# Attention scores from two rounded fp32 parts, with even and odd heads in the two halves of the array's rows

## The reference

```
x      = layernorm(input)                       # before the attention
Q,K,V  = x @ Wq.T + bq, x @ Wk.T + bk, x @ Wv.T + bv
scores = Q K^T / sqrt(16) + prior_lambda * mask(|i - j|)   # mask is a band, cut at 59 off the diagonal
attn   = softmax(scores);  out = attn V
x1     = input + (heads joined) @ Wo.T + bo
```

## Time and profile before

| what | value |
|---|---|
| median of 3 runs | 6518.96 us (6516.07 to 6520.48) |
| the profiled execution | 6517.32 us, its span 6515.5 us, 1.8 us lie around it |
| PE busy | 6199.8 us, 95% |
| DVE busy | 5158.3 us, 79% |
| ACT busy | 3831.1 us, 59% |
| attention, its 1024 steps | about 123.6 to 3571.2 us of the span |
| PE's granted clock | 1.00 of 2.4 GHz in nearly all of it |

### The profile page before, as it was taken

The page is one execution under the profiler, slowest core; times in us unless marked ns, Lnnn a source line. Parts: engine busy times, 40 slices in busy tenths (PEclk is TensorE's granted clock), DMA queues, the critical chain, the costliest instruction groups (busy, mean ns, idle before and its releaser), DMA issues. The chain is left out here.

```text
span 6515.5 us, 109356 instructions
## 1 busy us (share of the span) xinstructions
PE 6199.8 (95%) x42144; PEld 3462.2 (53%) x42336; DVE 5158.3 (79%) x10993; ACT 3831.1 (59%) x6282; POOL 1584.7 (24%) x1131
## 2 busy tenths in 40 slices
PE   7999999999999999999999799999899899999899
PEld 2333233333332333333322588888788688888788
DVE  6888888888888888788886788888666788888666
ACT  2665665666656656656666466666333566666332
POOL 0000000000000000000000577777200577777211
PEclk7999999999999999999999899999999899999999
DMA  1111111111111111111100100000000100000111
GB/s 47 20 25 28 20 25 42 22 32 19 28 36 22 29 29 19 25 38 24 24 16 9 48 15 13 15 15 10 26 12 4 33 15 15 13 15 9 54 49 43
DMA packets 150862, 160.14 MB, mean 25 GB/s; under 512 B 26268, under 2 KB 135620, under 8 KB 150340
## 3 DMA queue, kind: packets, MB, share of 16 engines
q1 hardware_dynamic: 150340, 153.14, 10.1%
HBM read 68.38 MB, written 16.78 MB: 13 GB/s over the span
## 5 line engine op out<-in xcount | busy, mean ns | idle before, releaser
L548 ACT ACTIVATE a_pr<-a_w 128x1024 f32<-128x1024 f32 x2048 | 2076.4, 1023 | 1124.9 <-PE a_w L423 800.2
L678 DVE TENSOR_REDUCE a_mx<-a_b 128x1 f32<-128x512 f32 x2688 | 1739.5, 684 | 332.0 <-PE a_b L407 312.6
L407 PE MATMUL a_b<-a_kp,a_qp 96*128 96x512 bf16 x4096 | 1449.9, 388 | 120.4 <-DVE a_mx L678 47.8
L423 PE MATMUL a_w<-a_qp,a_kp 99*128 99x512 bf16 x4096 | 1224.7, 380 | 32.6 <-ACT a_pr L548 32.5
L676 DVE CUSTOM_DVE_ANT_0 a_junk<-a_b,a_gw 128x512 bf16<-128x512 f32 x1408 | 964.4, 685 | 230.3 <-PE a_b L407 195.8
L454 PE MATMUL a_po<-a_pr,a_v 128*17 128x512 f32 x8192 | 1068.3, 595 | 0.5 <-ACT a_pr L548 0.5
L407 PEld LDWEIGHTS a_b<-a_kp,a_qp 96*128 96x128 bf16 x4096 | 339.7, 97 | 1238.5 <-issue 656.9
L1398 POOL TENSOR_TENSOR l_p<-l_p,l_rc 128x512 f32<-128x512 f32 (+1 forms) x512 | 633.0, 1260 | 450.7 <-DVE l_rc L1311 450.7
L1205 ACT ACTIVATE l_p<-l_S,l_nm 128x256 f32<-128x256 f32 (+1 forms) x1024 | 467.1, 465 | 458.6 <-DVE l_nm L1303 458.6
L423 PEld LDWEIGHTS a_w<-a_qp,a_kp 99*128 99x128 bf16 x4096 | 388.1, 98 | 513.9 <-ACT a_pr L548 108.8
L1054 PE MATMUL l_G<-l_wqkv,l_hT 128*128 128x512 f32 x2304 | 607.4, 409 | 21.8 <-DVE l_wqkv L1343 9.3
(11 more groups left out here) (164 smaller groups left out, 8302.8 us busy)
## 6 DMA issues: line engine op xcount, KB each, us to landing
a_xc<-in_x SPq DMA_DIRECT2D x60, 512.0 KB
a_qp<-a_qs SPq DMA_DIRECT2D x384, 64.0 KB, 2.4
a_kp<-a_ks SPq DMA_DIRECT2D x384, 64.0 KB, 2.4
l_tab<-in_rotary SPq DMA_DIRECT2D x128, 128.0 KB, 2.1
x<-a_xc SPq DMA_DIRECT2D x16, 512.0 KB, 2.9
f_xo<-x SPq DMA_DIRECT2D x16, 512.0 KB
out<-xs SPq DMA_DIRECT2D x16, 512.0 KB, 3.2
l_sh<-xs SPq DMA_DIRECT2D x32, 224.0 KB
```

The lines of the kernel that those rows point to most:

```text
L407: eng.matmul(bk, qp[s][0:96, qb * 128:qb * 128 + 128], kp[s][0:96, c * 512:c * 512 + 512], start=True, stop=True).then_inc(full, 1)
L423: m = eng.matmul(wide[u][:, c * 512:c * 512 + 512], kp[s][0:99, kb * 128:kb * 128 + 128], qp[s][0:99, u * 1024 + c * 512:u * 1024 + c * 51 ...
L548: eng.activation(pr[(2 * n + u) % NP][:, :], wide[u][:, :], ACT.Exp, scale=0.25).then_inc(s_exp[u], 1)
L678: t = eng.tensor_reduce(mx[g % 2][:, qb, c:c + 1], banks[i], X, ALU.max)
```

## The change

q and k are split into two fp32r parts instead of three bf16 parts. Three products (`QPART`, `KPART`) make 48 contraction rows, and 50 with the two rows of the negated maximum. Heads alternate between partitions 0 to 63 and 64 to 127 of the operand buffers (`operands(g)`), of which there are now two pairs of 128 rows, which hold four heads. PE's order alternates one pass-1 matmul and one pass-2 matmul; the unit stands in the middle of the step, and `band` and `pv` at its end.

`project` is ACT (fp32 copy with bias), ACT (the same, rounded to fp32r) and POOL (the difference), and then a DMA of 512 KB to a DRAM tensor that keeps the parts of all heads of all batches. `pack(g)` reads from there by 6 DMAs of 128 KB. x is loaded, normalized and turned once per batch; from that one pass come the values and all four projections of a chunk. The units of the next batch are spread from step 32 of the batch on, one about every fourth step. The first batch's projections of both groups of heads all stand before the steps.

```diff
-QPART = [0, 1, 2, 0, 1, 0]
-KPART = [0, 0, 0, 1, 1, 2]
+QPART = [0, 0, 1]
+KPART = [0, 1, 0]
...
+ROWS = 3 * DA
...
+def chunk_units(b, j):
+
+    return ([("turned", b, j, half) for half in range(2)] + [("values", b, j, half) for half in range(2)]
+            + [("project", b, c, j, n) for c in range(2) for n in "qk"])
...
-        n = n0 + 85
-        for j in range(4):
-            for what in (("turned", b, 1, j, 0), ("turned", b, 1, j, 1), ("project", b, 1, j, "q"), ("project", b, 1, j, "k")):
-                n = plan(n, *what)
...
-            n = n0 + 114
+            n = n0 + 32
             for j in range(4):
-                n = plan(n, "stats", b + 1, j) + 2
...
+                n = plan(n, "stats", b + 1, j) + 3
+                for what in chunk_units(b + 1, j):
+                    n = plan(n + 3, *what) + 1
...
-    parts = {"q": sb("qs", [128, 3, L], BF16), "k": sb("ks", [128, 3, L], BF16)}
-    qp = [sb(f"qp{i}", [128, L], BF16) for i in range(3)]
-    kp = [sb(f"kp{i}", [128, L], BF16) for i in range(3)]
+    parts = {n: nc.dram_tensor(n + "_parts", [NB, 2, 2, 128, L], F32, kind="Internal").ap() for n in "qk"}
+    stage = [sb(f"stage{i}", [128, 2, 512], F32R) for i in range(2)]
+    qp = [sb(f"qp{i}", [128, L], F32R) for i in range(2)]
+    kp = [sb(f"kp{i}", [128, L], F32R) for i in range(2)]
...
+    def operands(g):
+
+        return qp[g // 2 % 2], kp[g // 2 % 2], 64 * (g % 2)
...
         def pass1(n, c):
...
-                pe.wait_ge(s_pack[s], PACK * (g // 3 + 1))
-                eng.matmul(bk, qp[s][0:96, qb * 128:qb * 128 + 128], kp[s][0:96, c * 512:c * 512 + 512], start=True, stop=True).then_inc(full, 1)
...
+                pe.wait_ge(s_pack[g % 4], PACK * (g // 4 + 1))
+                eng.matmul(bk, q[r:r + ROWS, qb * 128:qb * 128 + 128], k[r:r + ROWS, c * 512:c * 512 + 512], start=True, stop=True).then_inc(full, 1)
...
         for n in range(-LEAD, NS + 1):
-            pass1(n, 0)
-            pass2(n, halves_of(n)[0])
-            pass1(n, 1)
-            pass2(n, halves_of(n)[1])
-            pass1(n, 2)
+            for c in range(2):
+                pass1(n, c)
+                pass2(n, halves_of(n)[0], c)
+            if n in units and units[n][0] in work:
+                work[units[n][0]](units[n])
+            for c in range(2):
+                pass1(n, c + 2)
+                pass2(n, halves_of(n)[1], c)
             band(n)
             pv(n - 1)
-            if n in units and units[n][0] in work:
-                work[units[n][0]](units[n])
-            pass1(n, 3)
...
+            act.wait_ge(s_full[i], k)
+            if m > 2:
+                act.wait_ge(s_lo, m - 2)
+                act.wait_ge(s_part[(m - 1) % 2], 16 * ((m - 1) // 2))
+            eng.activation(tmp[(m - 1) % 2][:, :], banks[i], ACT.Identity, bias=bias[n][:, c:c + 1]).then_inc(s_whole, 1)
+            eng.activation(stage[(m - 1) % 2][:, 0, :], banks[i], ACT.Identity, bias=bias[n][:, c:c + 1]).then_inc(s_free[i], 1)
...
-                dve.wait_ge(s_dve, step.on(eng.tensor_tensor(r1[:, :], nm[:, :], pk[:, 0, :], ALU.subtract)))
-                dve.wait_ge(s_dve, step.on(eng.tensor_copy(pk[:, 1, :], r1[:, :])))
-                eng.tensor_tensor(pk[:, 2, :], r1[:, :], pk[:, 1, :], ALU.subtract).then_inc(s_pk, 1)
+                eng.tensor_tensor(pk[:, 1, :], nm[:, :], pk[:, 0, :].bitcast(F32), ALU.subtract).then_inc(s_pk, 1)
...
+            eng.dma_start(parts[n][b, c, :, :, j * 512:j * 512 + 512].rearrange("t p n -> p t n"), stage[(m - 1) % 2][:, :, :].bitcast(F32)).then_inc(s_part[(m - 1) % 2], 16)
...
+            for n, dst, order in (("q", q, QPART), ("k", k, KPART)):
                 for j, p in enumerate(order):
-                    eng.dma_start(dst[16 * j:16 * j + 16, :], parts[n][r0:r0 + 16, p, :]).then_inc(s_pack[s], 16)
+                    eng.dma_start(dst[r + 16 * j:r + 16 * j + 16, :].bitcast(F32), parts[n][b, h // 8, p, r0:r0 + 16, :]).then_inc(s_pack[g % 4], 16)
```

More of the change, by code:

```diff
@@ L196, in unit @@
             return
[L197 removed]
+        if (what[0] == "turned" and what[3] == 0) or (what[0] == "out_T" and what[2] % 4 == 0):
             n_hT += 1
@@ L212, in attention_tables @@
     for half in range(2):
-        tick("normed", ("turned", 0, "v", 0, half))
+        tick("normed", ("turned", 0, 0, half))
     for j in range(4):
[L215 to L218, removed]
+        of_chunk = chunk_units(0, j)
+        for what in of_chunk:
             unit(what, 7)
@@ L222, in attention_tables @@
             for half in range(2):
-                tick("normed", ("turned", 0, "v", j + 1, half))
-        for what in held:
-            rest(what)
+                tick("normed", ("turned", 0, j + 1, half))
+        for what in of_chunk:
+            if what[0] in HOLDS:
+                rest(what)
     before_main = list(t.n)
@@ L245, in attention_tables @@
                 after = units[n]
[L246 to L249, removed]
+        for c in range(2, 4):
+            if p1:
+                t.take(("p1", g1, qb, c), 3)
+        if p1 and qb == W - 1:
+            later.append(("rows", g1))
         if n > 0 and n % W == 0:
@@ L471, in tensor @@
         for j in range(4):
-            for half in range(2):
-                turned(("turned", 0, "v", j, half))
-            for half in range(2):
-                values(("values", 0, j, half))
-            for n in "qk":
-                project(("project", 0, 0, j, n))
+            for what in chunk_units(0, j):
+                work[what[0]](what)
         pe.wait_ge(s_ones, 1)
@@ L509, in turned @@
         def turned(what):
-            half = what[4]
+            half = what[3]
             i, k = slot[what]
@@ L746, in vector @@
                 for half in range(2):
-                    normal(("turned", 0, "v", j + 1, half))
-            for n in "qk":
-                project(("project", 0, 0, j, n))
-        dve.wait_ge(s_setup, 3)
+                    normal(("turned", 0, j + 1, half))
+        dve.wait_ge(s_setup, 2)
         after = norm = None
@@ L807, in gpsimd @@
                 rstd(rs[:, 4 * j + 4:4 * j + 8], 4)
-            for n in "qk":
-                project_lo(("project", 0, 0, j, n))
+            for what in chunk_units(0, j):
+                if what[0] == "project":
+                    project_lo(what)
         after = None
@@ L894, in sync @@
         for j in range(4):
-            turned(("turned", 0, "v", j, 1))
+            turned(("turned", 0, j, 1))
+            for what in chunk_units(0, j):
+                if what[0] == "project":
+                    project(what)
+        sp.wait_ge(s_ones, 1)
         pack(0)
@@ L905, in sync @@
             if after:
-                store(after)
-                norm, after = after, None
+                if after[0] == "project":
+                    project(after)
+                else:
+                    store(after)
+                    norm = after
+                after = None
             if n in units:
```

192 lines of the change are left out of this document (75 added, 117 removed).

## The result

The changed kernel takes 6562.4 us, the median of 7 runs (6551.68 to 6605.92); the kernel before, measured beside it, takes 6518.7 us, the median of 7 (6516.07 to 6520.48). The ratio is 1.0076, with a 95% interval of 1.0052 to 1.0101: slower, where I forecast 6265 and faster. The time lies inside the range of 6110 to 6600, but on the wrong side of 6519: that it lies there is no merit of the mechanism. The profiled execution's span is 6560.6 us, 45.1 above that of before.

What follows compares the result with a forecast made beforehand. PE's stream was taken as the bound, with DVE close. From 6517.3 us, plain heads -119, units -107, output units -19 and work before the steps -8 gave 6264, stated as 6265; range 6110 to 6600.

Steps and rivals of the forecast that it cites:

- the halves overlap: Score matmuls in rows 0 to 63 and 64 to 127 run at the same time; plain heads shorten, -119 us.
- DVE releases the loop: In plain steps, a loop from DVE's first chunk through the three banks becomes the bound, 2.70 us a step.
- The extras: Per head, waits at the change of halves and the turns of maxima and finished head: 2.3 us kept as 2.4.
- Weights at nothing: In score matmuls, fp32r weight loads of 0.188 us against bf16's 0.10 stay hidden, so the difference costs nothing.
- before the steps: Ahead of the attention steps, eight more projections and their stores add +15 us, ends +8 and +25.
- The forecast sum of 41 us for a spread set: The next batch's units in the steps cost 41 us a set, 36 less than before; three times, -107 us.
- the sentence on new waits: ACT's two projection copies after both exponentials delay the next ones about 0.7 us, inside slack; all waits zero, up to +20.
- My own sign of being wrong: Wrong if pairs start 0.23 apart, ACT bounds the step, or a project unit costs more than 1.5 us.
- The worst case of the forecast: In the spread sets, each unit costs its present 1.5 us and only 16 dropped turned a batch gain: -38 us.
- the first rival: The halves of the rows don't overlap, every step is 2.99 us: 6585 us, slower; chance 0.17.
- the clock, given 0.04: In the steps, PE rests and its clock falls; with a third of steps slow, 6630 us; chance 0.04.
- the output sets: The 16 output units stay together and cost 29 us a set instead of 35.3: -19 us, ends 0 and -40.

Runs made afterwards that it cites:

- The inline kernel: Changed kernel, but ACT and DVE take a unit's result from its bank within the same step and the bank is not held over; 6440.0 us, ratio 0.988.
- the kernel with ACT's part alone: Changed kernel, but only ACT takes a unit's result between the two exponentials; DVE's takes and the holding of banks stay; 6539.6 us, ratio 1.0031.
- the second experiment: Changed kernel, but PE repeats a 50-row pass-2 matmul before each of the third and fourth pass-1 matmuls; 6756.3 us, ratio 1.0375.
- in the first: Changed kernel, but consecutive heads lie in the same half of the rows and every second pair of heads in the other; 6822.1 us, one run.
- consecutive steps: Changed kernel, but the next batch's units stand in consecutive steps instead of every fourth; 6528.8 us, ratio 1.0014.
- the two together: The inline kernel with the next batch's units in consecutive steps; 6439.7 us, ratio 0.9876.
- unit at the end: Changed kernel, but the unit stands behind pv at the end of PE's step instead of in the middle; 6520.8 us, ratio 1.0005.
- inline, whole array: The inline kernel plus two bf16 matmuls of 512 columns on all 128 rows in eleven of a head's steps; 6706.9 us, ratio 1.0289.
- inline, half array: The inline kernel plus two repeats of the 50-row pass-2 matmul in eleven of a head's steps; 6479.8 us, ratio 0.9938.

## Why the prediction was wrong, point by point

**Right: the halves overlap, and DVE releases the loop.** Pairs start together. A plain step is 2.75 (forecast 2.70), the last key block with both matmuls in one half 3.08 (2.99), a plain head 47.1 (46.5). The extras are 2.1 instead of 2.4. That rows overlap at all was taken without a row that showed it, and it came true in full. The last 0.05 is in the loop's small terms: 0.43 instead of 0.41 from the fourth pair to `band`, 0.17 instead of 0.16 from DVE to the pair. Weights at nothing was right, in a same-half stretch too: 0.23 between matmuls with their loads between. Only the first pair after `pv` took 0.11 more, outside the loop. This part gave 83 of the forecast 119 us.

**Right in kind: before the steps.** +18.5 us against +15, inside 8 to 25.

**Wrong: the units, the largest term.** The forecast sum of 41 us for a spread set priced a unit's own step only. The medians at full clock, over a plain step:

| unit | count | forecast | own step | step behind | measured |
|---|---|---|---|---|---|
| project | 16 | 1.2 | 1.55 | 0.45 | 2.0 |
| values | 8 | 1.6 | 1.6 | 1.5 | 3.1 |
| turned | 8 | 0.5 | 1.0 | 0.8 | 1.8 |
| stats | 4 | 1.3 | 0.45 | 1.2 | 1.6 |

They sum to 32 + 25 + 14 + 6 = 77.6 us, just what the kernel before paid for its unit sets (76.8). (Three of the four stats stand in the step behind a projection, so that some 1 us of the sum is counted twice.) Three sets miss by 110 us, about 90 of it in the steps behind. The step that failed is the sentence on new waits, that ACT's two copies come behind both exponentials "inside their slack": they delay no exponential much, but hold one of three banks over the step's end, and pass 1 needs it. The same holds of values, which DVE takes in the next step: the forecast priced them at 1.6 in all, and they cost 3.1. My own sign of being wrong, a project unit above 1.5 us, came true with 2.0. The inline kernel takes the steps behind projections, values and `turned` down to plain ones, and the kernel with ACT's part alone those behind projections and `turned`, and so they show the cause. The worst case of the forecast was also mis-summed: 16 dropped units at 1.5 us are 24 a batch, 72 us for three, not 38; the first rival's 6585 has the same 38.

**Wrong: the clock, given 0.04.** The sets measured 324 us where full clock makes 233, so 91 us are the clock's in these alone; with the output sets and single heads I put it at some 110 to 125, from some 80 steps with low clock, of which some 60 had no unit and took 4.4 us on average, where a plain step takes 2.75. My argument against it was that PE would be full at 1.2 GHz and that this would bring the clock back. The window 700 to 724 has PE busy all the time at 0.50, so it doesn't hold. My picture of the cause, PE resting, did not hold either: the second experiment filled most of the rests and had 342 us, and in the first the clock fell behind 15 us of which PE rested 0.7. The rival's size was guessed at a third of all steps; it was some 80 of 1024, and so turned the sign only together with the units.

The mean granted clock of every run confirms this size. The traces here have the two levels 0.50 and 1.00 only, so that it gives the time at 1.2 GHz in the whole execution, layers behind the attention included: 2 x (1 - clock) x span.

| kernel | runs | median us | at 1.2 GHz, median us |
|---|---|---|---|
| before (profiled run) | 1 | 6517.3 | 221 |
| changed | 7 | 6562.4 | 525 |
| both passes in one half | 1 | 6822.1 | 928 |
| more score matmuls | 4 | 6756.3 | 554 |
| inline | 4 | 6440.0 | 412 |
| ACT's part only | 10 | 6539.6 | 575 |
| consecutive steps | 10 | 6528.8 | 405 |
| the two together | 4 | 6439.7 | 412 |
| unit at the end | 10 | 6520.8 | 476 |
| inline, whole array | 4 | 6706.9 | 302 |
| inline, half array | 6 | 6479.8 | 395 |

The seven runs of the changed kernel are of one program, and their times follow the clock: from 6551.68 us (clock 0.961, 511 us low) to 6605.92 (0.950, 660 us low) it is 54 us for 149, so 0.36 us lost for each us at 1.2 GHz. The step above says the same: (4.22 - 2.75)/4.22 = 0.35. The runs of ACT's part only give 0.37 in the same way, those of consecutive steps 0.37. By this rate the 304 us more than before cost the changed kernel about 110 us, and of the inline kernel's 122 us the clock has 41 and the waits some 80. Since a clock is given to 0.001, each such figure is good to about 5 us.

**Wrong: the output sets.** 29 us forecast, 46 measured. A part is the held bank: inline, the step of an `out_project` at full clock falls from 5.5 to 4.5 us. A part is the clock: 9 of the 24 had the low clock, at 6.9 us. Inline, the sets still measured 42, 39 and 47 us, so the rest stays open.

**The account.** Plain heads -83 (61 at 1.36), units with their low clock +104 (462 against 358, each as what is left of the steps over plain heads), the last two heads +1, before the steps +18.5, behind the attention +4: the 45 us of the spans. Had the clock stayed as before, the changed kernel would, as an estimate by the rate above, have come out at about 6450, faster than before, though not at 6265.

**Open.** What makes the granted clock fall is not settled. Of the changed kernel's 39 falls, 37 begin in the step of a unit or in the step behind one, and 16 at key blocks 8 to 10, where the halves of the exponential change. Fewer waits at units (412 us inline) and work on all rows (302 us) went with less time at the lower level; unpaired matmuls in one half (928 us, one run) with more, and 50-row work in the gaps with about as much. That matmuls on few rows count less would fit these, but no experiment shows it: the whole-array kernel also filled PE's time more (3450 of 3610 us), and no run changed the rows alone. The split of the inline kernel's gain into waits and clock comes from medians and from the rate above, which agree (77 and 40, 80 and 41); no run had the one without the other, only the two heads shown.

## What to carry to other kernels

Price extra work by how long it holds its buffer, until the last reader of the bank is done, not by the time of the engine that fills it; with three banks in rotation, a result that is read at the end of the step costs the next step as well. Put the copy-out of a unit into its reader's idle time in the same step: here this turned +0.8% into -1.2%, two thirds by the waits and one third by the clock. And where a change makes each matmul smaller, look at the granted clock of the stretches with extra work before believing a gain that is counted at full clock.

## What the runs showed of the hardware

- Two fp32r matmuls of 48 and 50 rows in different halves of the array's rows start within 0.01 us and follow at 0.23 as a pair. In the same half each takes 0.23 for itself, and a step 3.11 instead of 2.75 (2925.64 to 2928.76).
- The first pair after work on all rows takes 0.34 instead of 0.23, and a 128-row matmul between two pairs 0.64 in all.
- At 1.2 GHz a step with paired halves took 4.22 us (722.11 to 726.33) against 2.75 at 2.4 GHz, and PE busy for 24 us on end didn't bring the clock back in that time.
- A kernel whose PE was recorded busy for 90% or more of the steps (3130 of 3462 us) can have a granted clock of 0.95, where the kernel before, busy for 96%, had 1.00; the clock also fell behind 15 us of which PE was recorded busy for 14.3.
- Between runs of one program, whose mean clock differed, each us at 1.2 GHz cost 0.36 us (6551.68 us at a mean clock of 0.961, 6605.92 at 0.950).
